# Post-norm vision tower: features 128 to 191 summed once, half-row products in pairs, V over four banks, another order of the step

## The chip, the cores and the metric

The kernel runs on one core of a Trainium2 chip. A core has five engines that run in parallel and wait for each other through semaphores: TensorE (PE, matrix products, with PEld for its weight loads), VectorE (DVE), ScalarE (ACT), GpSimd (POOL) and SyncE (SP, which issues most DMAs). SBUF is the on-chip memory of 128 partitions; PSUM, into which TensorE writes, has 8 banks (`ps[:, bank, ...]`). The metric is the time of one launch in microseconds (us), the median of several executions.

## The reference

64 images of 3x224x224 become 196 tokens of 192 features each, pass one attention block without softmax (12 heads of 16, causal decay) with a gate, and a soft mixture of 64 slots.

```python
h = einsum('bnk,dk->bnd', patches(x), W)                  # 196 tokens, 768 -> 192
q, k, v = silu(h @ Wq), silu(h @ Wk), silu(h @ Wv)        # 12 heads of 16
energy = einsum('bhnd,bhmd->bhnm', q, k) * decay          # decay = exp(slope * (n - m)), n >= m
out = einsum('bhnm,bhmd->bhnd', energy, v) * sigmoid(h @ Wg1 @ Wg2)
h = layernorm(h + layernorm(out @ Wo, ln_w, ln_b))
xn = rms_norm(h, norm_w)
logits = einsum('sd,btd->bst', l2(slots) * scale, l2(xn))
y = einsum('btd,bst->bsd', xn, softmax(logits, -1))       # over tokens
y = gelu(y @ fc1[s] + b1[s]) @ fc2[s] + b2[s]             # each slot its own weights
h = layernorm(h + einsum('bsd,bst->btd', y, softmax(logits, -2)))
```

## The kernel before, in words

The work has three stages. The first (`phase1`) goes over 32 pairs of images; the second over the 64 slots, two at a time, with their weights streamed from HBM; the third puts the slots' results together and writes the output. The change touches the first alone.

A step `i` of the first stage works on three pairs at once: part `a` embeds pair `i` and does its attention, part `c` does the output projection and first norms of pair `i - 1`, part `d` does the slot logits and softmaxes of pair `i - 2`. Steps 0 and 1 lack `d`, steps 32 and 33 lack `a`; steps 2 to 31 have all three. Every engine has its own `step` function, and the order of its calls is the order in which the engine works. There is no scheduler: an engine that reaches a wait stands until it is met.

Features 0 to 127 and 128 to 191 are handled apart. Products in 32-bit precision are made of three products of rounded halves (`product`: high by low, low by high, high by high; hTh is the rounded hT, hTl the rest). `embed(i, 1)` writes features 128 to 191 as two halves on 64 partitions each, whose sum is the value (products with the high and with the low half of W), and before the change no engine sums them: Q, K and V contract over all 128 partitions, with the weight rows of those features standing twice (`rows` in `kernel`), and `h_turned(i, 1)` sums them by `pick`.

The order on the engines around the change, for a full step:
- TensorE: `embed` 0, `project_out` 0, `token_features`, `embed` 1, `project_out` 1, `h_turned`, Q, V of the first image, K's first half, `logits`, K's second half, `scores` 0, `gate`, V of the second image, `keys_turned`, `logits_turned`, `scores` 1, `values` 0, `states`, `scores` 2, `values` 1, Es turned, `carried` 0, `slot_inputs`, `values` 2, `carried` 1, `combine_turned`, `slot_inputs_turned`.
- VectorE: `token_norms`, ogl, `first_norm`/`residual`/`residual_statistics` for half the tiles, hTl[1], the same for the other half with `cosine_scales` in it, hb (the embedded rows with the norm's bias, out of banks 6 and 7), zl, `cosines` (Lt, cmx, Lc), gn, `decay` 0, kts, `slot_maxima` (lneg), `decay` 1, state, `sums` (lrec, csum, crec), `decay` 2, `gated`.
- ScalarE copies and rounds hT, applies Silu to Q, K, V, then the squares, and the exponentials Es (which needs lneg) and Ec. GpSimd splits the next x, and computes powers (rstd, invn, ra) and xn.

`decay(i, k)` multiplies the scores in banks 2 to 5 by the decay table; `scores` k+1 waits for it (`p_rdy`), since the banks are the same, and `values` k reads its result. `logits` waits for `hb_sb`.

## Time and profile before

| what | value |
|---|---|
| median of 3 runs | 1220.85 us (1219.61 to 1221.07) |
| profiled execution, time | 1220.71 us |
| its span, first to last instruction | 1219.0 us |
| TensorE busy | 1105.5 us |
| VectorE busy | 787.8 us |
| ScalarE busy | 750.0 us |
| GpSimd busy | 595.9 us |
| mean granted TensorE clock | 0.958 |

The span is what the profile covers, some 1.7 us less than the execution's time. Busy is the sum of an engine's instructions with overlaps counted once; pipelined products overlap, so the distance from one start to the next says more of their cost than the duration of one. A line's "idle before" in brackets is the time for which the engine stood still ahead of it, with what released it.

### The profile page before, as it was taken

The numbers are of one execution on the slowest core, as the hardware profiler recorded it, in microseconds if no ns is written. First come the engines' busy times: TensorE is split into PE (matmuls) and PEld (weight loads), VectorE is DVE, ScalarE is ACT, GpSimd is POOL, SyncE is SP. The second block draws the span as 40 slices with busy tenths as digits, with TensorE's granted clock in tenths as the row PEclk, the third lists the DMA queues.
The fourth block names the chain that finished last, engine by engine and source line by source line (L and its number), as shares of the span: only waits on it lengthen the run. The fifth ranks groups of instructions, "written<-read, shape, count | busy, mean of one in ns | idle before, by whom it ended". The sixth has DMA issues, their size and how long they took to land.

```text
span 1219.0 us, 35974 instructions
## 1 busy us (share of the span) xinstructions
PE 1105.5 (91%) x13418; PEld 889.2 (73%) x13418; DVE 787.8 (65%) x2082; ACT 750.0 (62%) x1745; POOL 595.9 (49%) x942
## 2 busy tenths in 40 slices
PE   4899999999999999999999999999998999997563
PEld 3787888888888888888888888788886556564332
DVE  5577766677777777676777777777774222222996
ACT  5567677777777776777777777776763111110676
POOL 3366655565555666555655555665533000000664
PEclk9999999999999999999999999999999999998555
DMA  4411121111111111211111111112063999995786
GB/s 151 197 51 55 58 84 59 62 53 53 53 53 53 53 53 55 80 66 61 55 53 53 53 53 53 53 53 77 32 263 129 368 424 423 424 423 181 235 264 183
DMA packets 50718, 158.41 MB, mean 130 GB/s; under 512 B 5386, under 2 KB 31392, under 8 KB 38372
## 3 DMA queue, kind: packets, MB, share of 16 engines
q1 hardware_dynamic: 33080, 145.09, 32.2%
q10 hardware_dynamic: 17600, 12.78, 3.4%
q8 instruction: 28, 0.46, 0.2%
q14 instruction: 10, 0.08, 0.0%
HBM read 132.23 MB, written 25.62 MB: 129 GB/s over the span
## 4 chain that ended last, share of the span: by engine, by line
PE 71%; DVE 22%; issue 2%; ACT 1%; DVEq 1%; SPq 1%; DMA 1%; POOL 0%; ACTq 0%; POOLq 0%
DVE p_sb L828 9%; PE ps L974 8%; PE ps L976 7%; PE ps L975 7%; PE ps L1271 6%; PE ps L1052 5%; PE ps L1089 4%; PE ps L1290 4%; PE ps L1134 4%; DVE gn L803 3%; PE ps L1031 3%; PE ps L1032 3%; PE ps L1019 2%; PE ps L1157 2%; DVE res L943 2%
## 5 line engine op out<-in xcount | busy, mean ns | idle before, releaser
L427 POOL TENSOR_TENSOR xl<-x_sb,xh 128x392 fp32r<-128x392 f32 x192 | 189.8, 1026 | 84.1 <-DVE gn L803 74.9
L828 DVE TENSOR_TENSOR p_sb<-ps,dec 98x1568 f32<-98x1568 f32 x96 | 171.6, 1788 | 14.8 <-PE ps L1052 14.8
L678 ACT ACTIVATE hg<-ps 128x768 f32<-128x768 f32 x32 | 25.9, 810 | 146.0 <-PE ps L1295 146.0
L768 DVE BATCH_NORM_STATS2 st<-ps 98x6 f32<-98x192 f32 x128 | 40.0, 354 | 77.5 <-PE ps L1019 77.5
L935 DVE COPY y2st<-ps 128x192 f32<-128x192 f32 x32 | 11.4, 358 | 120.5 <-PE ps L1271 120.5
L695 ACT ACTIVATE o_sb<-res,nb,rstd 98x192 f32<-98x192 f32 x128 | 59.5, 535 | 44.8 <-DVE nb L958 44.1
L1089 PE MATMUL ps<-p_sb,vpad 98*32 98x98 f32 x3072 | 84.9, 250 | 1.6 <-DVE p_sb L828 1.6
L1319 PE MATMUL ps<-y2b,cbuf 64*98 64x192 f32 x256 | 49.3, 537 | 38.1 <-POOL y2b L532 38.1
L1089 PEld LDWEIGHTS ps<-p_sb,vpad 98*32 98x32 f32 x3072 | 64.1, 109 | 26.7 <-issue 26.2
L519 POOL CAST pickb<-pick 128x128 fp32r (+1 forms) x32 | 9.4, 293 | 148.8 <-PE ps L1295 148.8
L974 PE MATMUL ps<-xl,wh 128*128 128x392 f32 x192 | 70.1, 365 | 13.1 <-POOL xl L427 13.1
L446 POOL TENSOR_TENSOR hTl<-hT,hTh 128x392 fp32r<-128x392 f32 x32 | 32.6, 1018 | 97.9 <-ACT hTh L649 97.9
L563 ACT ACT_TABLE_LOAD x60 | 77.0, 1283 | 1.0
L786 DVE SCALAR_TENSOR_TENSOR t<-t,rstd,hb 98x192 f32<-98x192 f32 x128 | 60.5, 512 | 25.1 <-POOL rstd L483 25.1
L1319 PEld LDWEIGHTS ps<-y2b,cbuf 64*98 64x98 f32 x256 | 32.6, 266 | 54.6 <-issue 43.5
L568 ACT ACTIVATE xh<-x_sb 128x1176 fp32r<-128x1176 f32 x64 | 71.8, 1169 | 0.8 <-DMA x_sb<-in_xT 0.8
L1271 PEld LDWEIGHTS ps<-w2v,hgT 128*64 128x64 f32 x768 | 52.3, 137 | 25.9 <-issue 18.5
L1271 PE MATMUL ps<-w2v,hgT 128*64 128x192 f32 x768 | 69.5, 330 | 1.1 <-DVE hgT L929 1.1
L1031 PE MATMUL ps<-xl,whl 128*128 128x392 f32 x192 | 68.1, 355 | 0.0
L500 POOL TENSOR_TENSOR xn<-gn,ra 98x192 f32<-98x192 f32 x128 | 68.0, 560 | 0.0
L975 PE MATMUL ps<-xh,wl 128*128 128x392 f32 x192 | 66.5, 347 | 0.0
L976 PE MATMUL ps<-xh,wh 128*128 128x392 f32 x192 | 66.1, 344 | 0.0
(203 smaller groups left out, 3484.8 us busy)
## 6 DMA issues: line engine op xcount, KB each, us to landing
x_sb<-in_xT SPq DMA_DIRECT2D x32, 1176.0 KB, 5.2
w1v<-in_fc SPq DMA_DIRECT2D x32, 1152.0 KB, 10.2
w2v<-in_fc SPq DMA_DIRECT2D x32, 1152.0 KB, 12.7
h_dram<-h SPq DMA_DIRECT2D x32, 294.0 KB
h2r<-h_dram SPq DMA_DIRECT2D x32, 294.0 KB
out<-o_sb ACTq DMA_DIRECT2D x32, 294.0 KB
comb_dram<-cst SPq DMA_DIRECT2D x32, 98.0 KB, 1.7
cbuf<-comb_dram SPq DMA_DIRECT2D x32, 98.0 KB, 3.8
```

The costliest lines, as they stand in the source:

```text
L427: pool.tensor_tensor(xl[:, k], x_sb[:, k], xh[:, k].bitcast(F32), ALU.subtract)\
L500: pool.tensor_tensor(xn[0:T, t], gn[0:T, t], amp[:, t:t + 1].to_broadcast([T, D]), ALU.mult)\
L563: act.activation(warm[:, 1:2], warm[:, 0:1], func)
L568: act.activation(xh[:, c], x_sb[:, c], ACT.Copy).then_inc(xh_rdy, 1)
L828: dve.tensor_tensor(dst, src, rate.unsqueeze(2).to_broadcast([T, 4, 2, TOK]), ALU.mult)\
L974: pe.matmul(out, hi, x_lo, start=start, stop=False)
L975: pe.matmul(out, lo, x_hi, start=False, stop=False)
L976: return pe.matmul(out, hi, x_hi, start=False, stop=stop)
L1031: pe.matmul(ps[:, 1, 0:PT], whl[:, k], xl[:, k], start=(k == 0), stop=False)
L1089: mm = pe.matmul(ps[32 * r:32 * r + 32, 6 + k // 2, at:at + T], vpad[:, 2 * a + mt, 32 * h:32 * h + 32], p_sb[:, k % 2, mt, (2 * r + odd) ...
L1271: mm = pe.matmul(ps[64 * s:64 * s + 64, 4 + n % 2, 0:D], hgT[:, k, at:at + 64], w2v[n][:, s, k], start=(k == 0), stop=(k == FJ - 1))
L1319: mm = pe.matmul(ps[0:T, 2 * n + a, k * D:(k + 1) * D], cbuf[64 * a:64 * a + 64, n, k * T:(k + 1) * T], y2b[64 * a:64 * a + 64, n, :], sta ...
```

## The change

- The two halves of features 128 to 191 are added once (`summed_h`): ScalarE copies the lower half from PSUM to `kA[0:64]`, VectorE adds it twice, once for each 64 partitions of hT[:, 1], so that the sum stands on both halves. ScalarE rounds it as before.
- Q, K: the first half of the contraction is done for both groups of features, then the second half (64 rows) as pairs, one group on partitions 0 to 63, the other on 64 to 127. V the same with two token tiles as the pair, each image's V over two banks (4 and 5, 6 and 7). `h_turned(i, 1)` likewise.
- K comes before Q, both ahead of V and the logits; `gate` is ahead of `keys_turned` and behind the second image's V; `logits_turned` goes behind `states` with two transposes for four products; `carried` 0 ahead of Es turned, `values` 2 ahead of `slot_inputs`.
- gn is computed at the head of the next step (`tokens(i - 2)`), the squares follow tokT on ScalarE, into a tile of their own; `token_norms`, `cosine_scales`, `cosines`, zl, `slot_maxima` and GpSimd's `inverse_norms` move.
- The rounding of x is split in two on ScalarE, and GpSimd's split of x waits no more for gn. The output weights and the slots' rows are prepared at the end of step 0 and not ahead of it.

The core of the diff, in the order GpSimd, ScalarE, VectorE, TensorE; the functions `output_weights`, `slot_rows` and `slot_norms` hold statements that stood in front of step 0.

```diff
+            def slot_norms():
+                pool.wait_ge(sl_st, 1)
+                pool.tensor_tensor(slst[:, 1:2], slst[:, 0:1], expo[0:S, 1, 0:1], ALU.pow).then_inc(sl_st, 1)
+                pool.wait_ge(sl_st, 2)
+                pool.tensor_scalar(slst[:, 1:2], slst[:, 1:2], EPS, None, ALU.max).then_inc(sl_st, 1)
 
             def step(i, a, c, d, d_before, more):
-                if d:
-                    inverse_norms(i - 2)
...
                     first_norm(i - 1, 1)
+                if d:
+                    inverse_norms(i - 2)
                 if a:
                     pool.wait_ge(q_sb, 2 * i + 1)
                     qa = qA[:, :, :].rearrange("p b (a c m) -> p b a c m", a=2, c=2)[:, :, :, 1]
...
-                if d:
+                if d and a:
                     second_norm(i - 2)
                 if a:
-                    turned_h(i, 0)
+                    turned_h(i)
                 if d:
                     act.wait_ge(tokT_mm, i - 1)
                     act.activation(tokT[:, :, :], ps[0:G, 6:8, 0:PT], ACT.Copy).then_inc(tokT_sb, 1)
-                if a:
+                    if a or c:
+                        squares(i - 2)
+                    if not a:
+                        second_norm(i - 2)
+                if a:
+                    act.wait_ge(hT_mm, 2 * i + 2)
+                    act.activation(kA[0:64, :], ps[64:128, 1, 0:PT], ACT.Copy).then_inc(hlo_sb, 1)
+                    act.wait_ge(hx_rdy, 2 * i + 2)
+                    act.activation(hTh[:, 1], hT[:, 1], ACT.Copy).then_inc(hTh_rdy, 1)
                     use_table(ACT.Silu)
-                    turned_h(i, 1)
-                if more:
-                    for k in range(2):
-                        round_x(i + 1, k)
-                if a:
+                    if more:
+                        round_x(i + 1, 0)
+                    act.wait_ge(k_mm, 2 * i + 1)
+                    act.activation(kA[:, :], ps[:, K_AT, 0:PT], ACT.Silu).then_inc(k_sb, 1)
+                    act.wait_ge(k_mm, 2 * i + 2)
...
                     act.wait_ge(q_mm, 2 * i + 1)
...
+                    act.wait_ge(v_mm, 2 * i + 1)
+                    act.activation(vpad[:, 0:2].rearrange("p t (j q d) -> p t j q d", q=4, d=HD)[:, :, :, 0:4:3, :],
+                                   ps[0:T, V_AT[0]:V_AT[0] + 2, 0:D].rearrange("p t (j q d) -> p t j q d", q=2, d=HD),
+                                   ACT.Silu).then_inc(v_sb, 1)
...
+                    if more:
+                        round_x(i + 1, 1)
...
+            def squares(j):
+                for t in range(4):
+                    act.wait_ge(gn_rdy, 4 * j + t + 1)
+                    act.activation(ysq[:, t], gn[0:T, t], ACT.Square, accum_out=ss[:, t:t + 1]).then_inc(ss_rdy, 1)
...
+            def summed_h(i):
+                dve.wait_ge(hlo_sb, i + 1)
+                for x in range(2):
+                    dve.tensor_tensor(hT[64 * x:64 * x + 64, 1], ps[0:64, 1, 0:PT], kA[0:64, :],
+                                      ALU.add)                        .then_inc(hx_rdy, 1)
...
                 if d:
-                    token_norms(i - 2)
+                    mean_shifts(i - 2)
                 if c:
                     for g, n in enumerate((slice(0, PT), slice(PT, COLS))):
                         dve.wait_ge(ogh_rdy, 2 * i - 1 + g)
                         dve.tensor_tensor(ogl[:, n], og[:, n], ogh[:, n].bitcast(F32), ALU.subtract)\
                             .then_inc(ogl_rdy, 1)
+                if d and (a or c):
+                    tokens(i - 2)
+                if c:
                     first_norm(i - 1, 0)
                     residual(i - 1, 0)
+                if a:
+                    summed_h(i)
+                if c:
                     residual_statistics(i - 1, 0)
                 if a:
                     dve.wait_ge(hTh_rdy, 2 * i + 2)
@@ -878,10 +911,12 @@
                 if c:
                     first_norm(i - 1, 1)
                 if d:
-                    cosine_scales(i - 2)
+                    token_norms(i - 2)
                 if c:
                     residual(i - 1, 1)
                     residual_statistics(i - 1, 1)
+                if d:
+                    cosine_scales(i - 2)
...
                         .then_inc(hb_sb, 1)
-                    dve.wait_ge(q_sb, 2 * i + 2)
-                    dve.tensor_tensor(zs[ZL:ZL + RANK, :], ps[DB:DB + RANK, 1, 0:PT], zs[0:RANK, :].bitcast(F32),
+                if d:
+                    cosines(i - 2)
+                if a:
+                    dve.wait_ge(zh_rdy, 2 * i + 2)
+                    dve.tensor_tensor(zs[ZL:ZL + RANK, :], ps[DB:DB + RANK, Q_AT + 1, 0:PT], zs[0:RANK, :].bitcast(F32),
                                       ALU.subtract).then_inc(zl_rdy, 1)
...
-                    cosines(i - 2)
-                if c:
+                if c and not a:
                     tokens(i - 1)
...
+                    decay(i, 1)
                     if d:
                         slot_maxima(i - 2)
-                    decay(i, 1)
...
+            def project(i, bank, hi, lo, done, more=0):
+                groups = (slice(0, DA), slice(DA, D + more))
+                pe.wait_ge(hTl_rdy[0], i + 1)
+                for g, m in enumerate(groups):
+                    product(ps[0:m.stop - m.start, bank + g, 0:PT], hi[:, 0, m], lo[:, 0, m], hTh[:, 0], hTl[:, 0],
+                            True, False)
+                pe.wait_ge(hTl_rdy[1], i + 1)
+                for w, h in ((hi, hTl), (lo, hTh), (hi, hTh)):
+                    for g, m in enumerate(groups):
+                        rows = slice(64 * g, 64 * g + 64)
+                        mm = pe.matmul(ps[0:m.stop - m.start, bank + g, 0:PT], w[rows, 1, m], h[rows, 1],
+                                       start=False, stop=(w is hi and h is hTh))
+                        if w is hi and h is hTh:
+                            mm.then_inc(done, 1)
...
             def rows_of_v(i, a):
...
+                def at(mt):
+                    return ps[0:T, V_AT[a] + mt, 0:D]
+
+                for mt in range(2):
+                    n = slice((2 * a + mt) * T, (2 * a + mt + 1) * T)
+                    product(at(mt), hTh[:, 0, n], hTl[:, 0, n], wvh[:, 0], wvl[:, 0], True, False)
+                for h, w in ((hTh, wvl), (hTl, wvh), (hTh, wvh)):
+                    for mt in range(2):
+                        rows, n = slice(64 * mt, 64 * mt + 64), (2 * a + mt) * T
+                        mm = pe.matmul(at(mt), h[rows, 1, n:n + T], w[rows, 1],
+                                       start=False, stop=(h is hTh and w is wvh))
                 mm.then_inc(v_mm, 1)
...
-                pe.wait_ge(k_sb, 2 * i + 2)
+                pe.wait_ge(q_sb, 2 * i + 2)
+                pe.wait_ge(zl_rdy, i + 1)
...
-                pe.wait_ge(k_sb, 2 * i + 2)
-                pe.wait_ge(hb_sb, i + 1)
+                pe.wait_ge(v_sb, 2 * i + 2)
...
-                    for a in range(2):
-                        mm = pe.matmul(ps[64 * a:64 * a + 64, 0, k * T:(k + 1) * T],
-                                       Lt[0:T, 2 * a + k, :], ident[0:T, 0:T], start=True, stop=True)
+                    mm = pe.transpose(ps[:, 0, k * T:(k + 1) * T], Lt[0:T, 2 * k:2 * k + 2, :], ident[0:T, 0:T])
...
+                else:
+                    pe.wait_ge(hx_rdy, 2 * i + 2)
+                    for mt in range(2):
+                        for a in range(2):
+                            rows, at, n = slice(64 * a, 64 * a + 64), mt * D + 128, (2 * a + mt) * T
+                            mm = pe.matmul(ps[0:T, 6 + a, at:at + 64], hT[rows, 1, n:n + T],
+                                           ident[rows, rows], start=True, stop=True)
                     mm.then_inc(ht_mm, 1)
...
                         pe.wait_ge(t1_rdy, 4 * i - 2)
+                    project(i, K_AT, wkh, wkl, k_mm)
+                    project(i, Q_AT, wqh, wql, q_mm, more=RANK)
+                    if c:
+                        pe.wait_ge(t1_rdy, 4 * i)
                     rows_of_v(i, 0)
                 if d and not a:
                     idle_products(1, 12 if c else 2)
                     logits_turned(i - 2)
                 if a:
-                    pe.wait_ge(q_sb, 2 * i + 1)
-                    project(i, 0, wkh, wkl, k_mm)
+                    pe.wait_ge(hb_sb, i + 1)
                     if d:
-                        pe.wait_ge(hb_sb, i + 1)
                         logits(i - 2)
-                    pe.wait_ge(q_sb, 2 * i + 2)
-                    pe.wait_ge(zl_rdy, i + 1)
-                    project(i, 1, wkh, wkl, k_mm)
                     scores(i, 0, c)
-                    gate(i)
-                    pe.wait_ge(hb_sb, i + 1)
                     if d:
                         pe.wait_ge(Lt_rdy, i - 1)
                     rows_of_v(i, 1)
+                    gate(i)
                     keys_turned(i)
+                    scores(i, 1, c)
+                    values(i, 0)
+                    states(i)
                     if d:
                         pe.wait_ge(g_sb, 2 * i + 1)
                         logits_turned(i - 2)
-                    scores(i, 1, c)
-                    values(i, 0)
-                    states(i)
                     scores(i, 2, c)
-                    if not d:
-                        carried_ready(i)
+                    carried_ready(i)
                     values(i, 1)
                 if d:
+                    if not a:
+                        idle_products(1, 16 if c else 4)
                     if a:
-                        carried_ready(i)
-                    else:
-                        idle_products(1, 16 if c else 4)
+                        carried(i, 0)
                     dispatch_turned(i - 2)
                     if not a:
                         idle_products(1, 2)
                 if a:
-                    carried(i, 0)
+                    if not d:
+                        carried(i, 0)
+                    values(i, 2)
...
                     slot_inputs(i - 2)
                 if a:
-                    values(i, 2)
                     carried(i, 1)
...
+                if at_start(i):
+                    slots_turned()
```

What stands on VectorE between the first residual of a step and the one of the other half, before (st, mv: statistics; hTl: the low half of hT):

```order
L786 SCALAR_TENSOR_TENSOR t<-t,rstd,hb 98x192 [waits t1_rdy] x2
L792 BN_STATS st<-t 98x6 [waits t2_rdy] x2
L795 BN_AGGR mv<-st 98x2 x2
L875 REGISTER_ALU
L876 TENSOR_TENSOR hTl<-hT,hTh 128x392 [waits hTh_rdy]
L766 REGISTER_ALU
```

And now, in the changed program:

```order
L803 SCALAR_TENSOR_TENSOR t<-t,rstd,hb 98x192 [waits t1_rdy] x2
L842 REGISTER_ALU
L844 TENSOR_TENSOR hT<-ps,kA 64x392 [waits hlo_sb]
L844 TENSOR_TENSOR hT<-ps,kA 64x392
L809 BN_STATS st<-t 98x6 [waits t2_rdy] x2
L812 BN_AGGR mv<-st 98x2 x2
L908 REGISTER_ALU
L909 TENSOR_TENSOR hTl<-hT,hTh 128x392 [waits hTh_rdy]
```

Two additions that wait for ScalarE's copy (`hlo_sb`) have come in between.

Later in VectorE's step, from kts to the third decay (p_sb), before:

```order
L905 TENSOR_TENSOR kts<-ps,kdec 98x384 [waits kt_mm]
L853 TENSOR_REDUCE lneg<-ps 128x1 [waits lt_mm]
L823 REGISTER_ALU
L828 TENSOR_TENSOR p_sb<-ps,dec 98x4x2x196 [waits sc_mm]
L913 TENSOR_TENSOR state<-ps,parity 128x96 [waits s_mm]
L857 RECIPROCAL lrec<-lsum 128x1 [waits Es_rdy]
L859 TENSOR_REDUCE csum<-Ec 98x4 [waits Ec_rdy]
L861 RECIPROCAL crec<-csum 98x4 [waits csum_rdy]
L823 REGISTER_ALU [waits val_mm]
L828 TENSOR_TENSOR p_sb<-ps,dec 98x4x2x196 [waits sc_mm]
```

And now:

```order
L941 TENSOR_TENSOR kts<-ps,kdec 98x384 [waits kt_mm]
L850 REGISTER_ALU
L855 TENSOR_TENSOR p_sb<-ps,dec 98x4x2x196 [waits sc_mm]
L880 TENSOR_REDUCE lneg<-ps 128x1 [waits lt_mm]
L949 TENSOR_TENSOR state<-ps,parity 128x96 [waits s_mm]
L884 RECIPROCAL lrec<-lsum 128x1 [waits Es_rdy]
L886 TENSOR_REDUCE csum<-Ec 98x4 [waits Ec_rdy]
L888 RECIPROCAL crec<-csum 98x4 [waits csum_rdy]
L850 REGISTER_ALU [waits val_mm]
L855 TENSOR_TENSOR p_sb<-ps,dec 98x4x2x196 [waits sc_mm]
```

lneg has moved behind the second decay; the reciprocals and sums, which wait for exponentials made from it, still stand ahead of the third.

On TensorE, the end of a full step before (p_sb,vpad is `values`, qd,state `carried`, xn,DT `slot_inputs`):

```order
L1157 MATMUL ps<-xn,DT 64x192 [waits DT_sb,xn_rdy,g_sb]
L1157 MATMUL ps<-xn,DT 64x192 x3
L1083 REGISTER_ALU [waits s_sb]
L1089 MATMUL ps<-p_sb,vpad 32x98 [waits p_rdy]
L1089 MATMUL ps<-p_sb,vpad 32x98 x15
L1103 MATMUL ps<-qd,state 32x98 x4
L1118 MATMUL ps<-ident,Cn 128x98 [waits Cn_rdy]
```

And now:

```order
L1138 MATMUL ps<-p_sb,vpad 32x98 [waits p_rdy]
L1138 MATMUL ps<-p_sb,vpad 32x98 x15
L1204 MATMUL ps<-xn,DT 64x192 [waits DT_sb,xn_rdy,g_sb]
L1204 MATMUL ps<-xn,DT 64x192 x3
L1152 MATMUL ps<-qd,state 32x98 x4
L1167 MATMUL ps<-ident,Cn 128x98 [waits Cn_rdy]
```

`slot_inputs` is now behind the wait for the third decay (`p_rdy`).

## Rows read from the trace of the kernel before

**Rows 1.** The page: busy time by engine.

```profile
PE 1105.5 (91%) x13418; PEld 889.2 (73%) x13418; DVE 787.8 (65%) x2082; ACT 750.0 (62%) x1745; POOL 595.9 (49%) x942
```

**Rows 2.** Timeline, TensorE: two steps' first products (start us, us, engine, line, operation).

```profile
406.06 0.45 PE L974 MATMUL ps<-xl,wh 128*128 128x392 f32 x1
...
434.02 0.45 PE L974 MATMUL ps<-xl,wh 128*128 128x392 f32 x1
```

**Rows 3.** Timeline, TensorE: from `project_out` 0 to the logits.

```profile
409.83 0.25 PE L976 MATMUL ps<-woh,ogh 128*98 128x192 f32 x1
410.01 0.33 PE L1019 MATMUL ps<-wol,ogh 64*98 64x192 f32 x2
...
410.46 0.88 PE L1125 MATMUL ps<-ident,gn 98*96 98x98 f32 x8
...
414.91 0.83 PE L1168 MATMUL ps<-pick,hT 128*98 128x64 f32 x8
415.54 0.43 PE L974 MATMUL ps<-hTl,wqh 128*128 128x392 f32 x1
...
417.77 0.25 PE L974 MATMUL ps<-wvl,hTh 128*98 128x192 f32 x1
...
418.83 0.36 PE L974 MATMUL ps<-hTl,wkh 128*128 128x392 f32 x1
...
419.93 1.54 PE L1134 MATMUL ps<-slT,tokT 96*98 96x64 f32 x16
```

**Rows 4.** Timeline, TensorE: from `logits_turned` to the step's end.

```profile
425.27 0.56 PE L1142 MATMUL ps<-ident,Lt 98*64 98x98 f32 x8
...
428.75 0.92 PE L1052 MATMUL ps<-qB,kB 32*98 32x196 f32 x16 [0.91 <-DVE p_sb L828]
...
431.41 0.87 PE L1157 MATMUL ps<-xn,DT 98*64 98x192 f32 x8
...
433.03 0.37 PE L1103 MATMUL ps<-qd,state 32*32 32x98 f32 x8
```

**Rows 5.** Timeline, VectorE: statistics to hb, and the idle time before `wo_mm`.

```profile
413.86 0.60 DVE L792 BATCH_NORM_STATS2 st<-t 98x6 f32<-98x192 f32 x2
...
414.70 0.55 DVE L876 TENSOR_TENSOR hTl<-hT,hTh 128x392 fp32r<-128x392 f32 x1
415.17 0.62 DVE L768 BATCH_NORM_STATS2 st<-ps 98x6 f32<-98x192 f32 x2
...
418.86 0.96 DVE L889 TENSOR_TENSOR hb<-ps,lnb 98x768 f32<-98x768 f32 x1
...
438.54 0.63 DVE L768 BATCH_NORM_STATS2 st<-ps 98x6 f32<-98x192 f32 x2 [2.41 <-PE ps L1019]
```

**Rows 6.** Timeline, ScalarE: the second hT copy of the step.

```profile
413.62 0.47 ACT L647 ACTIVATE hT<-ps 128x392 f32<-128x392 f32 x1
```

**Rows 7.** Timeline, VectorE: cosines, gn and the three decays (p_sb).

```profile
421.51 0.42 DVE L842 TENSOR_TENSOR Lt<-ps,cosc 98x256 f32<-98x256 f32 x1 [0.43 <-PE ps L1134]
...
422.76 1.40 DVE L803 SCALAR_TENSOR_TENSOR gn<-t,mv,nw 98x192 f32<-98x192 f32 x4
424.08 1.78 DVE L828 TENSOR_TENSOR p_sb<-ps,dec 98x1568 f32<-98x1568 f32 x1
...
426.90 1.79 DVE L828 TENSOR_TENSOR p_sb<-ps,dec 98x1568 f32<-98x1568 f32 x1 [0.31 <-PE ps L1052]
...
429.74 1.79 DVE L828 TENSOR_TENSOR p_sb<-ps,dec 98x1568 f32<-98x1568 f32 x1
```

**Rows 8.** Timeline, VectorE: lneg and crec in step 33.

```profile
933.60 0.35 DVE L853 TENSOR_REDUCE lneg<-ps 128x1 f32<-128x196 f32 x1
...
935.29 0.18 DVE L861 RECIPROCAL crec<-csum 98x4 f32<-98x4 f32 x1
```

**Rows 9.** Windows: stretch, length, busy by engine (instructions), granted clock, DMA share, GB/s.

```profile
915.00:920.00 5.00, 3.65 (x35) 3.46 (x33) 4.53 (x17) 0.00 (x0) 2.62 (x6) 1.00 0.96 346
...
1140.00:1160.00 20.00, 11.67 (x60) 7.56 (x60) 18.63 (x75) 14.11 (x31) 13.54 (x23) 0.50 0.86 261
```

More of the change, by code:

```diff
@@ L64 @@
 SC_AT = 2
-V_AT = (2, 7)
+K_AT, Q_AT, V_AT = 2, 0, (4, 6)
 LG_AT = 2 * D
@@ L617, in step @@
                     last.then_inc(g_sb, 1)
-                    turned_v(i, 1)
-                if c:
-                    squares = h2 if a else hb
-                    if a and not (isinstance(i, int) and i == 1):
-                        act.wait_ge(h2_stored, 16 * (i - 1))
-                    for t in range(4):
-                        act.wait_ge(gn_rdy, 4 * (i - 1) + t + 1)
-                        act.activation(squares[0:T, t], gn[0:T, t], ACT.Square, accum_out=ss[:, t:t + 1]).then_inc(ss_rdy, 1)
+                elif c:
+                    squares(i - 1)
                 if d:
```

155 lines of the change are left out of this document (68 added, 87 removed).

## The prediction

> **What bounds the kernel now.** I read the page first: TensorE is busy 91% of the span [rows 1]. Then I laid out one step of the loop over image pairs in the timeline, engine by engine. The step shown starts on TensorE at 406.06 and the next one at 434.02, so a step takes 27.96 us, and there are 32 of them before the slots' part begins [rows 2]. Inside it TensorE runs almost without a gap: the only idle time shown is 0.91 us ahead of the third `scores`, which waits for VectorE's second `decay` [rows 4]. That makes TensorE look like the bound, but the reader should see how little VectorE has to give. `hb` starts at 418.86 and takes 0.96 us, so it is done at 419.82, and TensorE, which waits on `hb_sb` ahead of `logits`, starts them at 419.93 [rows 3, 5]. VectorE's chain from the first `wo_mm` to `hb` is already just in time. After it comes a second chain that goes to and fro: logits, cosines, `decay` 0, scores 1, `decay` 1, scores 2, `decay` 2, values 2. A step can be shortened only if both chains are.
>
> **What the change takes off TensorE.** The pairs on half the rows exist already in `project_out`: the last full product starts at 409.83, three pairs of 192 columns follow, and the next work starts at 410.46 [rows 3]. Full products of that width start 0.09 us apart (12 in 1.06 us, from 417.77 to 418.83), so the three pairs took 0.54 us, what six full products take: a fixed loss of some 0.27 us around them eats the saving [rows 3]. For V the saving is therefore nothing. With 392 columns a pair saves more and the fixed loss stays: the 12 products of Q take 2.23 us (415.54 to 417.77, with starts 0.178 apart, by estimate the slots' share of that stretch) [rows 3]; the new form takes 6 x 0.178 + 0.27 + 3 x 0.178 = 1.88. K and Q save 0.35 each, 0.7 a step. `logits_turned` (0.56 us) drops from four products to two, by estimate 0.3 [rows 4]; `h_turned` I take as unchanged (fewer slots, one more change of form). With the 0.91 us wait gone as well a step would be 27.96 - 0.7 - 0.3 - 0.91 = 26.0 us. That is TensorE's floor.
> The Trainium skill ("TensorEngine Tiling (Array Packing)", Theoretical Speedup and Key Properties) gives up to 2x for a contraction of 64 or less, and says that a change of tiling mode drains the engine. By the 2x alone K, Q and both V would save 2.1 us a step; this case's trace sides with the drain, 0.54 us where the 2x gives 0.27. Neither moves my forecast, since it is VectorE that TensorE will wait for.
>
> **What it puts on the chain to `hb`.** All on the clock of the step shown. `embed(i, 1)` ends as before, and ScalarE can copy its lower half at 413.62, as it copied hT then; 128x392 took 0.47 us [rows 6], so `hlo_sb` comes at 414.1. (The four `squares` now stand before that copy on ScalarE, behind tokT; by estimate, four of about 0.4 us from 412.2 on, they end just as it can start.) VectorE had `residual_statistics` at 413.86 [rows 5]; now it waits until 414.15 and does the two additions of `summed_h`. No row shows a 64x392 addition with one operand in PSUM; the nearest is hTl, 128x392 from SBUF, 0.55 us with 0.47 to the next start (414.70 to 415.17) [rows 5]. From 0.35 (a rate without the fixed part) to 0.6 each; I take 0.47. So statistics start at 415.1, 1.25 late. `token_norms` fits into the wait for `rstd` before the second `residual`; `cosine_scales`, which stood in that wait, now adds 0.1. `hb` starts at 420.2 and ends at 421.2. The gn products, moved to the step's head, fill 1.4 us of the 2.41 us that VectorE idles there before `wo_mm` [rows 5], at no cost.
> TensorE comes to `h_turned(i, 1)` at 414.9, waits for `hx_rdy` until 415.25, and then has 0.63 (414.91 to 415.54) + 2 x 1.88 + 1.06 ahead of the logits [rows 3]: it arrives at 420.7 and stands until 421.3. Before, K's second half was still behind the logits; now nothing is there to cover the wait.
>
> **What it does to the chain behind the logits.** Before, logits at 419.93 led to Lt at 421.51, so Lt is at 422.9. Cosines take 1.25 (421.51 to 422.76), then zl 0.47, and gn is gone (422.76 to 424.08, 1.32) [rows 7]. `decay` 0 starts at 424.6 instead of 424.08 and ends at 426.4. V and gate fit under it; TensorE is through keys at 425.8 and waits for `decay` 0 until 426.5, some 0.65 us. Scores take 0.92 [rows 4], so `decay` 1 starts at 427.45 (before: 426.90) and ends at 429.2.
> Now the step I weigh most. In the diff `slot_maxima` goes from ahead of `decay(i, 1)` to behind it, and `sums` still stands ahead of `decay(i, 2)`. Before, ScalarE's exponentials ran under `decay` 1, and from the start of `decay` 1 to that of `decay` 2 it was 2.84 us (426.90 to 429.74) [rows 7]. Now lneg, Es, Ec, csum, crec come one after the other on an idle VectorE. The last step of the stage shows just this sequence without cover: lneg at 933.60, crec at 935.29 [rows 8], 1.69 us, and 0.12 more to the next start. So 1.71 + 1.81 = 3.5 us from `decay` 1 to `decay` 2: it starts at 431.0 and ends at 432.8. Bounds: 0 if ScalarE's part somehow hides, 1.8 as in the rows less the 1.13 that VectorE spent there anyway; I take the rows.
> TensorE has done scores 2, values 1, carried and Es turned by 431.95 and waits until 432.85 for values 2. Then come values 2 and slot_inputs, which formerly lay in this gap, together 1.62 (431.41 to 433.03), the rest of the step, 0.99 (433.03 to 434.02) [rows 2, 4], and some 0.15 for ysb, now needed right after: 2.75. The next step starts at 435.6. **A step takes 29.55 us, 1.6 more than before.** TensorE's waits in it add to 3.5 us, and 26.0 + 3.5 agrees.
>
> **Ends.** 30 steps have all three parts (i = 2 to 31): +47 us. Step 0 gains about 3 us as weights are prepared later, and gives it back when `slot_rows` and `slots_turned` stand between it and step 1: 0, between -3 and +2. In the first step without new images `first_norm` waits for `second_norm`, which now stands behind tokT and squares: eight instructions of about the 0.47 us of [rows 6], so up to 4 late; the last step gains some by the reverse order. Together +2 (0 to 4). The slots' part and the output follow unchanged, and their weights are fetched against the same steps. Sum: 1220.7 (the profiled execution's time, 0.15 below the median of the runs) + 47 + 2 = 1270 us.
> POOL: splitting x loses its wait for gn but half of xh comes later; both end near 431, before TensorE needs them, so 0 (if the cover went, it would cost what it is late).
>
> **Rivals.**
> *Only one of the two chains bites* (the copy and additions take less, or the exponentials are covered). If `decay` 2 ended by 431.95, a step would be 28.65: +0.7 x 30 + 2, 1244 us. Against it: rows 8 show the sequence at full length. Chance 0.2, 1230 to 1250.
> *TensorE's floor rules; faster.* Place: `hb`. If it were ready at 420.7 or before and the sums covered, the step falls to between 26.0 and the same plus the old wait, 26.9: 59 to 32 us less, 1162 to 1189. It decides if the two additions together with their wait cost under 0.1 us more than VectorE's idle time and the sums nothing. For it: TensorE is busy 91%, VectorE far from it. Against it: `hb` was in time by 0.11 us only. Chance 0.12.
> *The granted clock falls.* TensorE now stands idle 3.5 us of a step in six places. In the output stage it was busy 58% and granted 0.50, the 1.2 GHz level; in the drain of this stage it was busy 73% and granted 1.00, 2.4 GHz [rows 9]. The new step would be busy 88%, on the side of the latter. If single steps fell to the lower level, each would cost several us: 1290 to 1400. Chance 0.08. The Trainium skill ("TensorE: Matmul & The Clock Gate", HAM oscillation) tells of kernels that fall back to the low clock in every wait; the trace so far does not agree for waits of 0.9 us, after which the clock stayed at 1.00.
> *It cancels*: losses of 1.0 to the floor's gain, within 0.2%. Chance 0.03.
>
> **How the numbers follow.** My forecast holds 0.57, with 1250 to 1288 for its own range (0.6 us a step either way on 30 steps). Faster by over 0.2% has 0.12 (the floor), within 0.2%, about what a measurement of this kernel can tell, 0.03, slower 0.85. The range must reach over the one-chain case and a little above the forecast: 1232 to 1292.
>
> **What would show it.** In the changed kernel's profile: a step of 29 to 30 us; TensorE idle ahead of logits, released by hb (0.6 each), ahead of scores 1 by p_sb (0.65), ahead of values 2 by p_sb (0.9); VectorE idle ahead of lrec and csum, released by Es and Ec; K's three pairs at 0.8 us. I am wrong if logits follow V without idle time, or if `decay` 1 to `decay` 2 is still 2.8 us.

## The result, and the profile after

| what | before | after |
|---|---|---|
| median | 1220.96 us (1219.61 to 1221.70, 4 runs) | 1286.09 us (1283.99 to 1288.23, 4 runs) |
| profiled execution, its span | 1220.71, 1219.0 us | 1287.03, 1283.8 us |
| one step of the loop | 27.96 us | 29.92 us |
| last full step ends, slots' part begins | 909.49, 938.22 | 970.07, 1002.50 |
| mean granted TensorE clock | 0.958 | 0.961 |

The change makes the kernel 1.0535 times as long [1.0514, 1.0556]: slower by 65 us, where 49 were forecast. The 30 full steps (1.96 us more in the one shown) are 58 us of it, steps 0 and 1 together 2.3, and the drain of the stage, its last two steps without new images, takes 32.4 us instead of 28.7. The clock has no part in the steps: it was granted at 1.00 throughout the full steps of both kernels. This line of the changed kernel's windows shows a part of them (stretch, length, busy time of PE, PEld, DVE, ACT and POOL, granted clock, DMA share, GB/s). In the drain of the changed kernel it fell to 0.50 for 3.4 us, behind a wait of 5.31 us for Lt; before, behind a wait of 1.98 us at that place, it did not.

```profile
600.00:700.00 100.00, 88.70 (x1261) 69.24 (x1257) 72.09 (x173) 67.70 (x159) 58.03 (x84) 1.00 0.17 57
```

Busy times on the page of the changed kernel, to set against [rows 1]: TensorE is busy for as long as before, VectorE for 37 us more.

```profile
PE 1106.4 (86%) x13226; PEld 835.5 (65%) x13226; DVE 824.7 (64%) x2146; ACT 753.1 (59%) x1745; POOL 600.7 (47%) x942
```

One step on TensorE in the timeline of the changed kernel (start us, us, engine, line, operation, and in brackets the idle time before it with its releaser). It answers to [rows 2 to 4]; before's clock is 4.23 us ahead of this one.

```profile
401.83 0.44 PE L1014 MATMUL ps<-xl,wh 128*128 128x392 f32 x1
...
411.10 0.56 PE L1219 MATMUL ps<-ident,hT 64*98 64x64 f32 x8 [0.26 <-DVE hT L844]
411.59 0.45 PE L1014 MATMUL ps<-hTl,wkh 128*128 128x392 f32 x1
...
412.86 0.44 PE L1028 MATMUL ps<-hTl,wkh 64*128 64x392 f32 x2
...
413.59 0.45 PE L1014 MATMUL ps<-hTl,wqh 128*128 128x392 f32 x1
...
415.58 0.34 PE L1014 MATMUL ps<-wvl,hTh 128*98 128x192 f32 x1
...
417.13 1.60 PE L1183 MATMUL ps<-slT,tokT 96*98 96x64 f32 x16 [0.33 <-DVE hb L924]
...
422.57 0.92 PE L1102 MATMUL ps<-qA,kA 32*98 32x196 f32 x16 [0.73 <-DVE p_sb L855]
...
425.41 0.92 PE L1102 MATMUL ps<-qB,kB 32*98 32x196 f32 x16 [0.59 <-DVE p_sb L855]
...
428.91 0.89 PE L1138 MATMUL ps<-p_sb,vpad 98*32 98x98 f32 x32 [0.93 <-DVE p_sb L855]
...
431.75 0.44 PE L1014 MATMUL ps<-xl,wh 128*128 128x392 f32 x1
```

Where before had one wait of 0.91 us in a step, there are now five, 2.84 us in all, and every one is released by VectorE. (A sixth, 0.12 us ahead of the gate's products, is too short for the timeline's brackets.) Two stretches of the same step on VectorE show how it comes to be late, for [rows 5] and [rows 7]:

```profile
409.90 1.15 DVE L844 TENSOR_TENSOR hT<-ps,kA 64x392 f32<-64x392 f32 x2 [0.20 <-ACT kA L593]
411.08 0.62 DVE L809 BATCH_NORM_STATS2 st<-t 98x6 f32<-98x192 f32 x2
...
416.12 0.96 DVE L924 TENSOR_TENSOR hb<-ps,lnb 98x768 f32<-98x768 f32 x1
418.76 0.42 DVE L869 TENSOR_TENSOR Lt<-ps,cosc 98x256 f32<-98x256 f32 x1 [1.69 <-PE ps L1183]
...
420.73 1.79 DVE L855 TENSOR_TENSOR p_sb<-ps,dec 98x1568 f32<-98x1568 f32 x1
...
423.56 1.79 DVE L855 TENSOR_TENSOR p_sb<-ps,dec 98x1568 f32<-98x1568 f32 x1 [0.58 <-PE ps L1102]
425.27 0.35 DVE L880 TENSOR_REDUCE lneg<-ps 128x1 f32<-128x196 f32 x1
...
426.20 0.16 DVE L884 RECIPROCAL lrec<-lsum 128x1 f32<-128x1 f32 x1 [0.42 <-ACT Es L666]
...
426.96 0.18 DVE L888 RECIPROCAL crec<-csum 98x4 f32<-98x4 f32 x1
427.06 1.79 DVE L855 TENSOR_TENSOR p_sb<-ps,dec 98x1568 f32<-98x1568 f32 x1
```

Measured from the step's first product, the logits start at 15.30 (before 13.87), decay 0 at 18.90 (18.02), decay 2 at 25.23 (23.68), and the step ends at 29.92 (27.96). So 1.43 us are lost ahead of the logits, 0.55 won back behind them because gn (1.32) no longer stands there, though zl (0.60) now does, 0.01 lost from decay 0 to 1, 0.66 from decay 1 to 2 (3.50 where it was 2.84), and 0.41 in the tail. That is a description and no cause yet: which edit holds which part is what the runs below are for. For most the length of a step is given too, read as above.

### The profile page after: what moved, and what is told of

Same layout as the page of the kernel before. It is cut to its first block, busy times and chain, and to the rows that moved or that the text cites. A ratio compares the mean times of both kernels' runs of the same rounds, so it can differ in the third digit from the quotient of the medians.

```text
span 1283.8 us, 35650 instructions
## 1 busy us (share of the span) xinstructions
PE 1106.4 (86%) x13226; PEld 835.5 (65%) x13226; DVE 824.7 (64%) x2146; ACT 753.1 (59%) x1745; POOL 600.7 (47%) x942
## 4 chain that ended last, share of the span: by engine, by line
PE 42%; DVE 37%; ACT 8%; issue 6%; DVEq 3%; SPq 1%; DMA 1%; ACTq 0%; POOL 0%; POOLq 0%
DVE p_sb L855 13%; PE ps L1317 5%; PE ps L1014 4%; PE ps L1183 4%; PE ps L1336 4%; ACT ysq L648 4%; PE ps L1015 3%; PE ps L1016 3%; PE ps L1102 3%; DVE hb L924 2%; PE ps L1138 2%; DVE res L983 2%; DVE st L809 2%; DVEq L810 2%; PE ps L1174 2%
## 5 line engine op out<-in xcount | busy, mean ns | idle before, releaser
L1102 PE MATMUL ps<-qA,kA 32*98 32x196 f32 x1024 | 58.9, 343 | 23.2 <-DVE p_sb L855 21.8
L571 ACT ACTIVATE xh<-x_sb 128x1176 fp32r<-128x1176 f32 x64 | 74.9, 1172 | 0.0
```

Source lines behind the costliest of these rows:

```text
L571: act.activation(xh[:, c], x_sb[:, c], ACT.Copy).then_inc(xh_rdy, 1)
L1102: mm = pe.matmul(ps[0:T, SC_AT + r, mt * TOK:(mt + 1) * TOK].rearrange("p (b n) -> p b n", b=2), keys[rows, n], queries[rows, :, n], start ...
```

## Experiments

**The sums of the exponentials (changed kernel).**

```diff
+                if a:
+                    decay(i, 2)
                 if d:
                     sums(i - 2)
                 if a:
-                    decay(i, 2)
```

> The changed kernel with sums (lrec, csum, crec) behind the third decay instead of ahead of it. Theory (exponentials exposed between the second and third decay): decay 2 starts as soon as scores 2 is done, 2.84 us after decay 1 instead of 3.50; values 2 and the step's end come 0.66 us earlier, 30 steps x 0.66 = 20 us off: 1266 us (1260 to 1272). Rival (the sums' place is covered by something else, the loss is all at hb): 1284 to 1288, no change.

Measured: 1267.43 us (1263.70 to 1271.18), 1.039 times before [1.0372, 1.0408]; a step is 29.26 us. TensorE's timeline:

```profile
420.52 0.88 PE L1139 MATMUL ps<-p_sb,vpad 98*32 98x98 f32 x32 [0.27 <-DVE p_sb L855]
```

The wait ahead of values 2 fell from 0.93 to 0.27, by just the 0.66 that decay 2 came earlier. The exposed sums cost 19 us.

**lneg where it was (changed kernel).** `slot_maxima` ahead of `decay(i, 1)` on VectorE, and `logits_turned` ahead of `scores(i, 1)` on TensorE, as before the change.

> The changed kernel with logits_turned ahead of scores 1 and slot_maxima ahead of decay 1, their places in the kernel before. Simple theory (only lneg's place counts): as with the sums last, 0.66 us a step, 1266 us. Rival, from the trace of the changed kernel: logits_turned needs g_sb, ScalarE makes it only at 422.7 since half of x's rounding now stands ahead of the tanh; scores 1 would go from 422.57 to 423.15 and decay 1 with it by 0.6, which gives back what is won: 1283 to 1287 us. I hold the rival likelier.

Measured: 1289.01 us (1284.91 to 1289.83), 1.0548 [1.0527, 1.0569]: nothing won. From decay 1 to 2 it was 2.84 us again, yet TensorE's timeline has a new wait ahead of scores 1:

```profile
424.39 0.39 PE L1190 MATMUL ps<-ident,Lt 98*128 98x98 f32 x2 [0.93 <-ACT gt L632]
...
427.54 0.92 PE L1102 MATMUL ps<-qB,kB 32*98 32x196 f32 x16 [0.91 <-DVE p_sb L855]
```

`logits_turned` writes the gate's bank and must wait until ScalarE has read it, and with K, Q, V and the rounding of x ahead of it ScalarE reads it late. By this the transposes can't go back unless ScalarE's order does; no run tried both.

That is only a part of the result. A step of this run is 29.77 us, 0.15 shorter than in the changed kernel, some 4 us over all steps. But in 8 of the 30 full steps the granted clock fell to 0.50 for 3.4 or 6.8 us, each time 0.4 to 0.7 us after the end of the new wait, and those steps took 30.41 to 31.60 us: 6.3 us lost. One of them, in TensorE's timeline and in windows:

```profile
454.14 0.39 PE L1190 MATMUL ps<-ident,Lt 98*128 98x98 f32 x2 [0.93 <-ACT gt L632]
454.46 1.50 PE L1102 MATMUL ps<-qA,kA 32*98 32x196 f32 x16
```

```profile
457.00:461.00 4.00, 3.89 (x88) 2.93 (x84) 3.06 (x6) 0.00 (x0) 3.83 (x6) 0.50 0.35 92
```

**Features 128 to 191 left in two halves (changed kernel).** ScalarE copies all of hT at once, `summed_h` is gone, and Q, K, V and `h_turned` contract over full rows as before; the rest of the new order stays.

```diff
-                    act.activation(kA[0:64, :], ps[64:128, 1, 0:PT], ACT.Copy).then_inc(hlo_sb, 1)
+                    act.activation(hT[:, 1], ps[:, 1, 0:PT], ACT.Copy).then_inc(hx_rdy, 2)
...
-                    summed_h(i)
```

> The changed kernel in its new order, with features 128 to 191 left as two halves: one ScalarE copy of 128x392, full products for K, Q and V, h_turned by pick; no additions on VectorE. Theory (in the new order TensorE itself comes to the logits only 0.3 us before hb is done, so the additions cost little): TensorE needs 0.23 us more for each of K and Q, 0.15 less for each V, the wait for hb goes; 0.1 to 0.3 us a step less, 1277 to 1284 us. Rival (the additions on the way to hb are the loss): 1.2 us a step, 1250 us.

Measured: 1271.66 us (1271.25 to 1272.24), 1.0415 [1.0398, 1.0433]; a step is 29.56 us. That is 14 us faster than the changed kernel, outside the range that I expected, and a long way from the rival's 1250. Of the 14, 10.8 are the 30 steps (0.36 each) and 1.8 steps 0 and 1. Neither wait for hb nor for hT is left, but the logits start 14.93 us into the step, still 1.06 later than before the change, which is six full products: K's second half, now ahead of them (hb is done at 13.93 and holds them no more).

**Two additions put into the kernel before.** They read and write scratch tiles, so that the result isn't touched, and stand where `summed_h` stands in the change:

```diff
                     residual(i - 1, 0)
+                    if a:
+                        for x in range(2):
+                            dve.tensor_tensor(spare[64 * x:64 * x + 64, :], cst2[0:64, :], cst2[0:64, :], ALU.add)
                     residual_statistics(i - 1, 0)
```

> The kernel before with two additions of 64x392 (SBUF only, into a tile nobody reads) on VectorE between residual and residual_statistics of the first half; nothing waits for them. Theory (in the kernel before, VectorE's chain to hb has only 0.1 us to spare): 2 x 0.47 - 0.1 = 0.85 us a step, 30 steps: 1246 us (1240 to 1250). Rival (TensorE bounds, VectorE has room): 1221 us, no change.

Measured: 1284.07 us (1282.87 to 1285.68), 1.0517 [1.0499, 1.0534]. The rival, slack on VectorE, is out; my number was 38 us too low. Timelines of VectorE and TensorE:

```profile
409.91 1.65 DVE L877 TENSOR_TENSOR spare<-cst 64x392 f32<-64x392 f32 x2
...
415.00 1.16 DVE L788 SCALAR_TENSOR_TENSOR t<-t,rstd,hb 98x192 f32<-98x192 f32 x2 [0.32 <-POOL rstd L484]
...
418.02 1.60 PE L1139 MATMUL ps<-slT,tokT 96*98 96x64 f32 x16 [0.96 <-DVE hb L894]
```

The pair took 1.65 us, and the second residual, pushed beside GpSimd's qd, 1.16 instead of 0.75. hb starts 14.91 us into the step instead of 12.80 [rows 5], and the step is 30.07 instead of 27.96: 2.11 us of delay, 2.11 us of step. TensorE already waits 0.65 us for hTl ahead of Q, then these 0.96 for hb, and the logits start 2.05 us later than before. The claim that VectorE's chain to hb has no slack is shown, nearly one to one (the slack of 0.11 aside); the price of the additions is another one than in the changed kernel.

**The drain (changed kernel).** In step 32 the second norm ahead of tokT, as in full steps.

> The changed kernel with second_norm ahead of the tokT copy in the first step without new images too (step 32), as in the kernel before; the last step keeps the new order. Theory: first_norm waits 4.07 us there for second_norm behind squares; 3.5 us of them come back: 1282.5 us (1281.5 to 1284). Rival (something else in the drain is late by as much): no change, 1286.

Measured: 1281.81 us (1280.80 to 1283.35, 5 runs), 1.05 [1.0485, 1.0514]: 4.3 us less than the changed kernel. The drain is 27.7 us long, 1.0 shorter than before the change. What it removes is this wait, in VectorE's timeline of the changed kernel:

```profile
978.23 0.74 DVE L796 SCALAR_TENSOR_TENSOR t<-ps,mv,lnw 98x192 f32<-98x192 f32 x2 [4.07 <-ACT h L655]
```

**Slot inputs ahead of values 2 (changed kernel).**

```diff
                     if not d:
                         carried(i, 0)
-                    values(i, 2)
                 if d:
                     if a:
                         pe.wait_ge(g_sb, 2 * i + 2)
                     slot_inputs(i - 2)
                 if a:
+                    values(i, 2)
                     carried(i, 1)
```

> The changed kernel with the next step's slot inputs taken ahead of the values of the slots 2 instead of behind them; nothing is left out of the computation. In the changed kernel TensorE waits 0.93 us there for decay 2 and then does the inputs behind values 2, and the step ends at 431.75. Theory (the tail is 0.41 us longer than before because the inputs stand behind the last values): the inputs fit into the 0.93 us in which TensorE waits for decay 2 anyway, values 2 start when they did, and the step is 0.5 to 0.7 us shorter: 1286 - 0.65 x 30 = 1267 us (1265 to 1271). Rival (the end of the step is held by the last product's consumer and not by TensorE's order): no change, 1286.

Measured: 1269.56 us (1267.14 to 1270.45), 1.0409 [1.0392, 1.0426]; a step is 29.33 us.

```profile
422.03 0.87 PE L1204 MATMUL ps<-xn,DT 98*64 98x192 f32 x8 [0.57 <-ACT DT L673]
422.83 0.89 PE L1138 MATMUL ps<-p_sb,vpad 98*32 98x98 f32 x32
```

TensorE now waits 0.57 us for DT instead of 0.93 for decay 2, and the inputs fill the rest.

**Both, the sums and the inputs.**

> The changed kernel with both edits: the sums of the exponentials behind decay 2, and the slot inputs ahead of values 2; nothing is left out. Theory: both live on the same wait of TensorE for decay 2 (0.93 us in the changed kernel, 0.27 us once the sums stand behind decay 2), so that the gains don't add up: 1265 us (1260 to 1270), the sums' 1267 and little more. Rival (the two are separate terms of the sum, 0.66 and 0.41 us in each of 30 steps): 1286 - 19 - 19 = 1248 us.

Measured: 1268.65 us (1266.63 to 1270.19), 1.0394 [1.0376, 1.0411]. 18.7 us and 16.5 us apart, 17.4 together; a step is 29.32 us, as with the inputs alone. TensorE's timeline:

```profile
423.03 0.87 PE L1205 MATMUL ps<-xn,DT 98*64 98x192 f32 x8 [0.56 <-ACT DT L673]
```

Each of the two edits takes away the wait for decay 2. With the inputs first the limit is DT, which ScalarE copies out of PSUM behind Es turned, and an earlier decay 2 doesn't make DT earlier. So the two terms of my division of the step don't add up.

**Three costs at once: sums, summation, drain.**

> The changed kernel with three of its costs taken away together: the sums of the exponentials behind decay 2, the features left as two halves with full products (the summation isn't done), and the second norm ahead of the transposed tokens in the last step; nothing is left out of the result. Theory (three separate terms): 1286 - 19 - 14 - 4 = 1249 us (1244 to 1254), still 28 us over the kernel before; what remains is the order alone, the projections ahead of the logits, some 0.9 us in each of 30 steps. Rival (the terms overlap on VectorE): 1262 or more.

Measured: 1248.33 us (1245.36 to 1248.81), 1.0226 [1.0209, 1.0243]; a step is 28.88 us. The sum of the three runs is 18.7 + 14.4 + 4.3 = 37.4, and 37.8 were measured: these are separate terms. 0.92 us a step are left, and the next three runs look for them in the order.

**In addition, Q's second half behind the logits.**

```diff
-                    project(i, Q_AT, wqh, wql, q_mm, more=RANK)
+                    group_of_q(i, 0)
...
                         logits(i - 2)
+                    group_of_q(i, 1)
                     scores(i, 0, c)
```

> The changed kernel with the three costs taken away as in the run before, and in addition the second half of Q (six products of 0.178 us each) behind the logits and not ahead of them, as the kernel before had the second half of K; nothing is left out of the result. Theory (what remains of the loss, 0.92 us a step, is the order): the logits start about 0.95 us earlier (the bias rows hb then become the limit at once), the cosines too, but zl needs the late half of Q, so decay 0 starts only 0.3 to 0.5 us earlier: a step of 28.4 to 28.6 instead of 28.88, 1248 - 0.4 x 30 = 1236 us (1232 to 1242). Rival (it isn't the place of the logits that costs, but something behind them): 1248, as without the edit.

Measured: 1324.37 us (1321.02 to 1328.45), 1.084 [1.0822, 1.0858]. Neither the theory nor the rival. The logits did move up: they start 1.01 us behind the start of hb (462.75 and 461.74) and no longer 1.96 (403.99 and 402.03 in the run before). But qB comes late, and behind it on GpSimd stand qd, six pieces of x's rounding error, the token scales and Cn. Timeline of TensorE, the end of one step and the start of the next, and windows of the same stretch:

```profile
443.51 0.37 PE L1151 MATMUL ps<-qd,state 32*32 32x98 f32 x8
445.16 0.59 PE L1166 MATMUL ps<-ident,Cn 98*128 98x98 f32 x2 [1.28 <-POOL Cn L510]
...
446.31 0.70 PE L1012 MATMUL ps<-xl,wh 128*128 128x392 f32 x1
446.80 0.53 PE L1013 MATMUL ps<-xh,wl 128*128 128x392 f32 x1
447.13 0.53 PE L1014 MATMUL ps<-xh,wh 128*128 128x392 f32 x1
```

```profile
446.00:449.00 3.00, 3.00 (x12) 2.88 (x13) 1.43 (x5) 2.67 (x8) 0.00 (x0) 0.50 0.45 178
449.00:452.00 3.00, 3.00 (x11) 3.00 (x11) 0.73 (x3) 0.55 (x2) 0.00 (x0) 0.54 0.32 100
452.00:455.00 3.00, 3.00 (x29) 2.78 (x28) 1.61 (x6) 1.94 (x4) 1.49 (x3) 1.00 0.00 0
```

From the end of the wait of 1.28 us on, TensorE works at a granted clock of 0.50, the 1.2 GHz level, for 6.6 us; products follow each other by 0.33 us and not by 0.18. The clock fell at this wait in 26 of the 30 full steps, for 3.4 or 6.8 us. The four steps without a fall took 29.7 to 30.1 us (two of them 29.89), the others 31.4 to 32.4. So of the 76 us over the run before, some 30 are the wait itself (1.0 in each step) and some 48 the clock.

**The same, with Cn ahead of the last piece of x on GpSimd.**

```diff
-                    split_x(i + 1, range(KP))
+                    split_x(i + 1, range(KP - 1))
+                if d:
+                    combine_weights(i - 2)
+                if more:
+                    split_x(i + 1, (KP - 1,))
```

> The run before (Q's second half behind the logits, 1324 us) with one edit on GpSimd alone: the combine weights Cn are computed ahead of the last of the six pieces of x's rounding error and not behind all of them and the token scales; nothing is left out. In the run before, TensorE waited 1.28 us for Cn near the end of the step, and the next step began at a granted clock of 0.50 to 0.54 for 5.5 us. Theory (the late Cn costs its wait, and the wait costs the clock): with Cn in time the clock stays at 1.00 and the step is near that without Q's move: 1244 us (1238 to 1252). Rival (the clock falls for the new order's other waits, or the pieces of x are late too): 1290 or more.

Measured: 1245.82 us (1244.63 to 1246.23), 1.02 [1.0182, 1.0218]. 79 us gone with one instruction moved on an engine that is busy 45% of the time. Windows, and a line of VectorE's timeline:

```profile
500.00:700.00 200.00, 190.43 (x2440) 159.46 (x2436) 140.34 (x363) 146.36 (x342) 112.85 (x167) 1.00 0.16 56
```

```profile
405.15 0.56 DVE L931 TENSOR_TENSOR zs<-ps,zs 16x392 fp32r<-16x392 f32 x1 [0.80 <-ACT zs L617]
```

The clock is at 1.00 in all full steps. TensorE still waits 0.49, 0.59 and 0.27 us in each step, so it was the wait for Cn and not those that cost the clock. This run also answers what the run before was made for: the logits start 13.99 us into the step and no longer 14.93, and yet a step is 28.84 us, against 28.88. zl now waits 0.80 us for the late half of Q, and decay 0 starts only 0.1 us earlier.

**The three costs away, zl behind decay 0 and the gate behind scores 1.**

> The changed kernel with the three costs taken away (1248 us), and in addition zl (the rounding error of the gate's inner rows) behind decay 0 instead of ahead of it on VectorE, and with it the gate's products behind scores 1 on TensorE; nothing is left out. Theory (what is left of the loss is that the decays stand late behind the logits, and TensorE waits for decay 0): decay 0 starts 0.59 us earlier, scores 1 and all that follows 0.6 us: 1248 - 0.6 x 30 = 1230 us (1226 to 1238). Rival (the last part of the step is held by TensorE's own work or by the slots' side): 1248.

Measured: 1246.10 us (1245.72 to 1251.49), 1.02 [1.0182, 1.0218]; a step is 28.83 us. The first part happened: scores 1 start 19.60 us into the step instead of 20.29, values 2 25.30 instead of 25.96. Then it is lost, in TensorE's timeline:

```profile
408.40 0.43 PE L1100 MATMUL ps<-ident,kA 128*98 128x128 f32 x2 [0.58 <-ACT vpad L624]
...
417.40 0.39 PE L1158 MATMUL ps<-ident,Cn 98*128 98x98 f32 x2 [0.85 <-POOL Cn L510]
```

Again Cn, with 0.17 us of wait without this edit. The decays' lateness is 0.4 us of what was left, but GpSimd's chain stands right behind it. In one of the 30 steps the granted clock fell to 0.50 for 3.4 us right behind the wait for Cn (0.84 us), which cost 1.5 us in two steps. Both edits together, zl late and Cn early, were not tried.

**Another order, built from the kernel before.** The features stay in two halves. gn is computed in halves behind decay 1 and behind `gated` 0, the squares go behind the exponentials, the sums behind decay 2, and `logits_turned` behind `states`; GpSimd's split of x no longer waits for gn.

```diff
+                if a:
+                    if c:
+                        tokens(i - 1, (0, 1))
+                    decay(i, 2)
                 if d:
                     sums(i - 2)
                 if a:
-                    decay(i, 2)
                     gated(i, 0)
+                    if c:
+                        tokens(i - 1, (2, 3))
```

> The kernel before with another order of the step and nothing of the summation: TensorE does scores 1, values 0 and states ahead of logits_turned; VectorE does decay 0 right behind the cosines, gn in two halves behind decay 1 and behind the first gated product, sums behind decay 2; ScalarE squares behind the exponentials; GpSimd's split of x waits no more for gn. Theory (the 0.91 us for which TensorE waits for decay 1 is all that the order can win, and it needs the decays earlier): the wait falls to about 0.25, 0.65 us a step, 1201 us (1195 to 1208). Rival (GpSimd's split now beside VectorE's SBUF-only work slows it, or a squared row comes late for the norms): 1215 to 1235.

Measured: 1201.96 us (1201.25 to 1202.57), 0.9847 [0.9832, 0.9862]: 1.5% faster than the kernel before. A step is 27.38 us, and one wait is left in it:

```profile
420.93 0.92 PE L1062 MATMUL ps<-qB,kB 32*98 32x196 f32 x16 [0.42 <-DVE p_sb L833]
```

The edits were made together; which of them brings how much of the 0.6 us is not shown.

## Why the prediction was right, and where its sizes were off

- **Direction and mechanism: right.** Both chains that it named bite. The hb chain has next to no slack (two additions in the kernel before: 2.11 us of delay, 2.11 us of step), and the exposed sums cost 0.66 us in each step (taking them away gives 19 us back). Forecast from decay 1 to decay 2: 3.5 us; measured: 3.50.
- **The step's clock times.** On before's clock, forecast and measured: copy done 414.1 and 414.09, statistics 415.1 and 415.31, hb done 421.2 and 421.31, logits 421.3 and 421.36, decay 0 424.6 and 424.96, decay 2 431.0 and 431.29, next step 435.6 and 435.98. The step was forecast 0.37 us too short, 11 of the 16 us by which the time was missed.
- **Terms that were mis-sized.** The two additions took 1.18 us to the next start and not 0.94; the price was taken from a 128x392 row out of SBUF [rows 5]. From Lt to decay 0 it was 1.97 (418.76 to 420.73) and not 1.72. The drain grew by 3.7 us, near the upper end given; step 0 was 0.9 longer and step 1 another 1.4, where the forecast had 0 for the start. TensorE's waits were put at 3.5 us a step and measured 2.84: that the step came out nearly right is owed to VectorE's chain, since "26.0 + 3.5 agrees" has both terms wrong, in opposite directions.
- **TensorE's saving: wrong.** K took 2.00 us (411.59 to 413.59) and Q 1.99, not 1.88 each, and V 1.22 (415.58 to the end of its work, 417.13 less the wait of 0.33), not 1.06. The fixed loss around a group of pairs of 392 columns is 0.40 (2.00 less nine slots of 0.178), where 0.27 was taken from the pairs of 192 columns in `project_out`: K's three pairs alone, 412.86 to 413.59, took 0.73 instead of 0.53. With full products in the same order (features left in two halves) K took 2.22, Q 2.15 and V 1.07, so the pairs save 0.22 and 0.16 and lose 0.15 in each V: 0.1 us a step. Over the whole step TensorE's own time, the step less its waits, is 29.92 - 2.84 = 27.08 us, and before it was 27.96 - 0.91 = 27.05. No run shows a floor of 26.0: `logits_turned` saved 0.26 as forecast, but the logits took 1.53 instead of 1.35, and the turned products at the step's end 0.93 instead of 0.69. This didn't touch the forecast, which followed VectorE's chain, but it did the rival: by this estimate the changed kernel with every wait gone would be at 1220.7 - 0.88 x 30 = 1194 us, not 1162. (The 2.1 us that the prediction works out for the 2x alone are 1.6 by its own distances: three starts of 0.178 saved in K and in Q, three of 0.09 in each V.)
- **What the forecast didn't see: two causes behind one delay.** It put the late logits down to the copy and the additions. Taking these away gave 0.36 us a step back and not 1.4, since K as a whole now stands ahead of the logits and holds them at 14.93 us anyway. Nor is the place of the logits a price by itself: with Q's second half behind them and Cn in time they start at 13.99, and the step is 28.84 us where it was 28.88. The prediction's step had both numbers (TensorE arrives at 420.7, hb ends at 421.2), and that they are close means that neither is the whole cause.
- **The tail.** Its 0.41 us are no term beside the sums: moving `slot_inputs` ahead of `values` 2 and moving the sums behind decay 2 both take away the same wait for decay 2 (17.4 us together, 18.7 and 16.5 alone), and behind it stands one of 0.56 us for DT.
- **Rivals.** One chain only: no, and its price was too low as well. It was put at 1244 us; with the sums taken away the kernel is at 1267, with the summation taken away at 1272. Floor: no. The clock: not in this kernel, whose longest wait in a full step is about 1 us; in one of the variants it fell in 26 of 30 steps, at a wait of 1.28 us, and that run took 1324 us, within the 1290 to 1400 of the rival. By the Trainium skill ("TensorE: Matmul & The Clock Gate", HAM oscillation) waits between bursts send the engine back to the low clock. This case agrees for the wait of 1.28 us, in part for one of 0.93 (8 of 30 steps with `logits_turned` put back), and not for the five of up to 0.93 in the changed kernel, which left the clock at 1.00.
- **Still open.** Of the 1.96 us, 0.66 are the sums and 0.36 the summation with its pairs (0.48 if all 14.4 us are put on the steps), both shown by runs. The rest, 0.92, goes with the order, and that is what is left when the other costs are taken away, not what a run has turned back: 0.42 of it is decay 0 that stands later (18.44 us into the step against 18.02), read from the trace; the other half lies behind decay 2. Three edits against it (Q's second half behind the logits, that with Cn in time, and zl late) left a step of 28.83 us or more.

## What to carry to other kernels

Where the busiest engine gets its input from another one just in time, as here, a saving on the busiest engine is worth nothing, and each microsecond added to the other's chain is worth a microsecond of every step: read the slack where the two meet (0.11 us here) before the busy shares. Two delays that end at the same wait don't add up, neither when they come nor when they are taken away; test them alone and together. An engine with half of its time free still holds a deadline: follow what is queued behind the instruction that you delay (qB, qd, six pieces, scales, Cn), up to the last consumer.

## What the runs showed of the hardware

- VectorE beside GpSimd: the 98x192 pair with all its tensors in SBUF took 1.15 us (median) beside GpSimd's xn, 1.16 beside its qd and 0.75 alone. The 64x392 additions took 0.56 us with one input in PSUM in each of 64 executions (0.556 to 0.559), 60 of them partly beside xn. With both inputs in SBUF, in the run with two additions put in, they took 0.78 to 0.86 in the 60 executions beside xn and 0.55 and 0.56 in the two without. By the Trainium skill ("SBUF — State Buffer", Who interferes with whom), a VectorE instruction with two SBUF inputs contends with a GpSimd instruction that reads SBUF, and one with at most one SBUF input does not; the trace agrees, with these numbers. So a duration measured out of SBUF holds only beside the same work on GpSimd.
- The clock: no single length of wait tells whether it falls. It fell to 0.50 for 3.4 or 6.8 us at a wait of 1.28 us in 26 of 30 steps, behind one of 0.93 us (for the gate, in the run with lneg where it was) in 8 of 30, and behind one of 0.84 us (Cn, with zl late) in 1 of 30. It stayed at 1.00 behind the 0.93 us ahead of values 2 in each full step of the changed kernel, behind the 0.91 us of the kernel before, and behind 1.98 us in that kernel's drain. What tells these apart is not shown. A fall of 3.4 us made a step 0.6 to 1.7 us longer.
